# Four graph attention layers: VectorE's neighbour sums through a PSUM bank, and ScalarE's row copy behind the next tile's norm

## The reference

```python
# --- layer 0 (adj_preln) ---
h = jnp.maximum(_layernorm(x, axis=-1), 0.0)
x = x + _L0_gnn_ref(h, adj, L0_gnn_W, L0_gnn_a)   # 4 heads: Wh = h @ W; softmax(leaky(s_i + s_j)) @ Wh; elu
h = jnp.maximum(_layernorm(x, axis=-1), 0.0)
x = x + _L1_gnn_ref(h, adj, L1_gnn_W, L1_gnn_a)   # 1 head: h @ W + softmax(...) @ h
h = jnp.maximum(_layernorm(x, axis=-1), 0.0)
x = x + _L2_gnn_ref(adj, h, L2_gnn_weights, L2_gnn_biases, L2_gnn_phis)   # 4 heads, biases, no elu
h = jnp.maximum(_layernorm(x, axis=-1), 0.0)
x = x + _L3_gnn_ref(h, adj, L3_gnn_Wq, L3_gnn_bq, L3_gnn_Wk, L3_gnn_bk, L3_gnn_Wv, L3_gnn_bv)   # q k v attention
```

## Time and profile before

| | us |
|---|---|
| median of 3 runs | 1858.07 |
| lowest and highest | 1850.53, 1858.45 |
| the profiled execution | 1857.89 |
| its span (first to last instruction) | 1856.1 |
| busy: GpSimd, VectorE, TensorE, ScalarE | 1183.0, 1276.6, 724.0, 638.4 |
| chain that ended last: GpSimd, issue, TensorE, VectorE | 53%, 18%, 9%, 8% |

### The profile page before, as it was taken

The page is one execution under the profiler, slowest core; times in us unless marked ns, Lnnn a source line. Parts: engine busy times, 40 slices in busy tenths (PEclk is TensorE's granted clock), DMA queues, the critical chain, the costliest instruction groups (busy, mean ns, idle before and its releaser), DMA issues.

```text
span 1856.1 us, 12880 instructions
## 1 busy us (share of the span) xinstructions
PE 724.0 (39%) x2660; PEld 407.7 (22%) x2660; DVE 1276.6 (69%) x2730; ACT 638.4 (34%) x2069; POOL 1183.0 (64%) x1201
## 2 busy tenths in 40 slices
PE   3565500112223312233345134555666233455354
PEld 2443300001111101111122011222222222334243
DVE  2887743978888929666778196677653639668684
ACT  6778500223334511112223123233333222423343
POOL 0000267777777777777777787777744654777774
PEclk9996555555555555555555566666666566776777
DMA  9999789444454464444455644455545665777773
GB/s 354 384 384 364 183 278 169 107 117 119 125 133 129 129 135 110 123 128 124 131 142 135 135 119 141 138 151 152 161 137 158 193 167 160 232 239 223 240 233 101
DMA packets 171212, 328.63 MB, mean 177 GB/s; under 512 B 39918, under 2 KB 82935, under 8 KB 171128
## 3 DMA queue, kind: packets, MB, share of 16 engines
q0 software_dynamic: 65920, 197.88, 39.4%
q1 hardware_dynamic: 82600, 104.48, 17.6%
q10 hardware_dynamic: 22608, 25.40, 4.0%
HBM read 288.94 MB, written 38.72 MB: 177 GB/s over the span
## 4 chain that ended last, share of the span: by engine, by line
POOL 53%; issue 18%; PE 9%; DVE 8%; ACT 6%; DMA 4%; SPq 1%; ACTq 1%; POOLq 0%; DVEq 0%
POOL s_ring L749 50%; PE ps L1575 3%; ACT s_a L804 2%; DMA s_adj<-in_adj_dram 2%; DMA s_ring<-s_tab,s_idx 2%; PE ps L1544 2%; POOL s_pay L736 1%; DVE s_sc L1286 1%; DVE s_ring L1284 1%; POOL out_dram L756 1%; PE ps L1580 1%; SPq L599 1%; PE ps L1600 1%; DVE s_ring L1395 1%; DVE s_ring L1399 1%
## 5 line engine op out<-in xcount | busy, mean ns | idle before, releaser
L749 POOL DMA_INDIRECT s_ring<-s_tab,s_idx x1104 | 1115.6, 1010 | 419.3 <-issue 337.3
L939 ACT ACTIVATE ps<-s_sc,s_least 128x9 f32<-128x9 f32 (+12 forms) x416 | 110.3, 265 | 701.5 <-DVE s_least L1272 461.1
L1395 DVE TENSOR_TENSOR s_ring<-s_ring,ps 128x2304 f32<-128x2304 f32 (+10 forms) x96 | 261.2, 2720 | 3.3
L1399 DVE TENSOR_TENSOR s_ring<-s_ring 128x512 f32<-128x512 f32 (+7 forms) x249 | 234.8, 943 | 8.6
L1555 PE MATMUL ps<-s_ident,s_hb 128*128 128x128 f32 x128 | 43.8, 446 | 415.9 <-ACT s_hb L895 359.9
L1600 PE MATMUL ps<-s_ring,s_ident 128*128 128x256 f32 x366 | 125.2, 511 | 202.9 <-DVE s_ring L1417 202.9
L736 POOL DMA_INDIRECT s_pay<-s_pay_t,s_rank_i x32 | 31.2, 974 | 223.0 <-DVE s_rank_f L1144 213.5
L1284 DVE TENSOR_TENSOR s_ring<-s_ring,ps 128x2304 f32<-128x2304 f32 (+12 forms) x32 | 87.1, 2721 | 123.6 <-DMA s_ring<-s_tab,s_idx 123.2
L1268 DVE SCALAR_TENSOR_TENSOR s_sc<-s_ring 128x36 f32<-128x36 f32 (+20 forms) x96 | 18.4, 192 | 186.9 <-DMA s_ring<-s_tab,s_idx 186.6
L1584 PE MATMUL ps<-s_wx,s_hT 128*128 128x258 f32 (+1 forms) x256 | 134.8, 682 | 30.9 <-ACT s_hT L904 29.8
L1600 PEld LDWEIGHTS ps<-s_ring,s_ident 128*128 128x128 f32 x366 | 92.6, 261 | 232.5 <-issue 214.4
(11 more groups left out here) (190 smaller groups left out, 1409.3 us busy)
## 6 DMA issues: line engine op xcount, KB each, us to landing
s_adj<-in_adj_dram SPq DMA_DIRECT2D x32, 2048.0 KB, 16.1
s_ring<-s_tab,s_idx POOLq DMA_INDIRECT x1104, 3.2
s_tab<-s_tb ACTq DMA_DIRECT2D x32, 256.0 KB, 2.5
s_ring<-s_tab SPq DMA_DIRECT2D x32, 256.0 KB, 3.7
s_ring<-s_pay SPq DMA_DIRECT2D x32, 132.0 KB, 2.3
s_tab<-s_tb ACTq DMA_DIRECT2D x32, 132.0 KB, 2.5
s_ring<-s_tab SPq DMA_DIRECT2D x32, 132.0 KB, 2.3
s_tab<-s_tb ACTq DMA_DIRECT2D x32, 129.0 KB, 2.4
```

The source lines that it names most:

```text
L749: e.indirect_dma_start(g[:, k, 0:L.row], None, table, bass.IndirectOffsetOnAxis(ap=self.idx[:, t, k:k + 1], axis=0)).then_inc(self.gat[n % ...
L939: m = e.activation(p[:, :, h], s[:, :, h], ACT.Exp, bias=self.least[:, j, h:h + 1], scale=-1.0, accum_out=self.total[:, j, h:h + 1])
L1395: e.tensor_tensor(v, v, wide(p, 3, L.hd), ALU.mult).then_inc(self.v)
L1399: e.tensor_tensor(g[:, 0:h, :], g[:, 0:h, :], g[:, c - h:c, :], ALU.add).then_inc(self.v)
```

## The change

`vec_sum` no longer adds by halves in SBUF. It multiplies the first two rows into PSUM bank 2 (`two`, 2 x 256), the others in place as before, and then adds the others to the bank, two rows (512 elements) at a time; an odd row is added alone. In layers 1 and 2 the bank's two halves stay apart and `vec_finish` adds each to `x`. In layer 0 three adds of 256 elements bring them together, since the elu needs the whole sum. On ScalarE `act_row(n-2)` moves behind `act_hidden(n-1)` and `act_turned(n-1)` in layers 0 to 2, and at a layer's end `act_turned(31)` goes ahead of `act_row(30)`.

```diff
     def total_y(self, L, n):
-        return self.half[:, n % 2, :] if L.n < 3 else self.bank(2 + n % 2, 0, D)
+        return self.bank(2 if L.n < 3 else 2 + n % 2, 0, D)
+
+    def two(self):
+        return self.bank(2).rearrange("p (k d) -> p k d", k=2)
...
-            if n > 1:
-                self.act_row(e, l, n - 2)
             if n:
                 self.act_hidden(e, l, n - 1)
                 self.act_turned(e, l, n - 1)
+            if n > 1:
+                self.act_row(e, l, n - 2)
         if l == 1:
             self.act_below(e, T - 1)
         if l < 4:
             self.act_hidden(e, l, T - 1)
+            self.act_turned(e, l, T - 1)
             self.act_row(e, l, T - 2)
-            self.act_turned(e, l, T - 1)
             self.act_row(e, l, T - 1)
...
-        v = g.rearrange("p k (h d) -> p k h d", h=L.heads)
-        e.tensor_tensor(v, v, wide(p, 3, L.hd), ALU.mult).then_inc(self.v)
-        while c > 2:
-            e.wait_ge(self.v, vs.up())
-            h = c // 2
-            e.tensor_tensor(g[:, 0:h, :], g[:, 0:h, :], g[:, c - h:c, :], ALU.add).then_inc(self.v)
-            c -= h
-        e.wait_ge(self.v, vs.up())
-        e.tensor_tensor(self.half[:, n % 2, :], g[:, 0, :], g[:, 1, :], ALU.add).then_inc(self.agg)
+        e.tensor_tensor(parted(two), parted(g[:, 0:2, :]), wide(p[:, 0:2], 3, L.hd), ALU.mult).then_inc(self.v)
+        vs.up()
+        v = parted(g[:, 2:c, :])
+        e.tensor_tensor(v, v, wide(p[:, 2:c], 3, L.hd), ALU.mult).then_inc(self.v)
+        vs.up()
+        if c % 2:
+            e.wait_ge(self.v, vs.n)
+            e.tensor_tensor(two[:, 0, :], two[:, 0, :], g[:, c - 1, :], ALU.add).then_inc(self.v)
+            vs.up()
+            c -= 1
+        for a in range(2, c - 2, 2):
+            e.wait_ge(self.v, vs.n)
+            e.tensor_tensor(two, two, g[:, a:a + 2, :], ALU.add).then_inc(self.v)
+            vs.up()
+        e.wait_ge(self.v, vs.n)
+        if L.n:
+            e.tensor_tensor(two, two, g[:, c - 2:c, :], ALU.add).then_inc(self.agg)
+            return
+        e.tensor_tensor(g[:, c - 1, :], two[:, 1, :], g[:, c - 1, :], ALU.add).then_inc(self.v)
+        e.tensor_tensor(two[:, 0, :], two[:, 0, :], g[:, c - 2, :], ALU.add).then_inc(self.v)
+        vs.up()
+        e.wait_ge(self.v, vs.up())
+        e.tensor_tensor(two[:, 0, :], two[:, 0, :], g[:, c - 1, :], ALU.add).then_inc(self.agg)
...
         elif L.n == 1:
-            e.scalar_tensor_tensor(x, y, self.total[:, n % 2, 0:1], x, ALU.mult, ALU.add).then_inc(self.x_new)
+            total = self.total[:, n % 2, 0:1]
+            e.scalar_tensor_tensor(x, y, total, x, ALU.mult, ALU.add).then_inc(self.v)
+            e.wait_ge(self.v, vs.up())
+            e.scalar_tensor_tensor(x, self.two()[:, 1, :], total, x, ALU.mult, ALU.add).then_inc(self.x_new)
+        elif L.n == 2:
+            e.tensor_tensor(x, x, y, ALU.add).then_inc(self.v)
+            e.wait_ge(self.v, vs.up())
+            e.tensor_tensor(x, x, self.two()[:, 1, :], ALU.add).then_inc(self.x_new)
```

More of the change, by code:

```diff
@@ L1388, in vec_sum @@
         vs, g, p = self.vs, self.rows(L, n)[:, :, 0:D], self.scores(L, n)[1]
-        c = KS[L.order[n]] + 1
+        c, two = KS[L.order[n]] + 1, self.two()
+        parted = lambda a: a.rearrange("p k (h d) -> p k h d", h=L.heads)
         if L.n == 1:
```

## The result

| | us | runs |
|---|---|---|
| before | 1857.61 median (1850.53 to 1858.45) | 4 |
| after | 1766.76 median (1766.33 to 1768.36) | 4 |
| ratio | 0.9521, 95% interval 0.9496 to 0.9545 | |
| the profiled execution of after | 1766.5, span 1764.7 | |

The account below looks back on a forecast made before the run. GpSimd's gathers, stalled by VectorE's two-SBUF-input adds, bound layers 1 and 2, VectorE layer 0, a ScalarE-TensorE loop layer 2's end. Layers 1, 2, 3 start 2.8, 23.7, 82.9 us earlier: 1857.9 - 82.9 = 1775 us, range 1762 to 1816.

Parts of the forecast that it names:

- The stall, and the gathers of 262 us: Layers 0 to 2: adds with two SBUF inputs stall gathers; with sums in PSUM, busy falls from 284-285 to near 262 us.
- Rival A: Gathers of layers 0 to 2: something other than the second SBUF input holds the port, stall stays; 1827 us, chance 0.08.
- Adds into PSUM at no extra cost: VectorE's 512-element adds into the bank: they stay near 0.69 us, 0 extra.
- rival B: VectorE's adds into PSUM cost 0.07 to 0.1 us more each; 1790 us, chance 0.13.
- rival D: VectorE's adds reading and writing the same bank take double, +0.53 us each; 1880 us, slower, chance 0.04.
- VectorE's +0.56 us a tile in layer 0: VectorE's sum in layer 0: added instructions and gaps make it longer, 19.6 us before tile 29.
- The start of a layer behind the copy of tile 27: Next layer's first gather: copy at most 5.9 us after tile 29's scores; layer 1 starts 2.8 us earlier, layer 2 23.7.
- The end of layer 2: Tail of layer 2: TensorE bounds it at 6.93 us a tile instead of 10.24; layer 3's gathers resume 82.9 us earlier.
- just in time: End of layer 2: GpSimd's 20 early gathers are done at 1357.6, before layer 3's gathers go on at 1359.2.
- Rival C: Tail of layer 2: a wait still ties the copy ahead of the norm, 10.24 us a tile; 1814 us, chance 0.05.

Follow-up runs that it names:

- sbuf_total_2: The changed kernel with its two running sums in an SBUF tile instead of a PSUM bank: 1796.66 us, ratio 0.9682 to the kernel before.
- order_27_2: The changed kernel with row copies ahead of the norm again in layers 0 and 1, and in layer 2 for tile 27 alone: 1760.43 us, ratio 0.9496.
- order_tail: The changed kernel with the row copy ahead of the norm again, except from tile 30 of layer 2 on: 1787.98 us, ratio 0.9643.
- sums_only: The changed kernel with ScalarE's order of before: ratios 1.0074, 1.0054 and 1.0022 on three chips where before takes 2139 to 2157 us.
- order_only: The kernel before with ScalarE's new order, sums still in SBUF: ratios 0.9789, 0.9789 and 0.9807 on three chips where before takes 2139 to 2157 us.

## Why the prediction was right

**The stall, and the gathers of 262 us: right.** Rival A is out, by after's windows and by `sbuf_total_2`. Of the seven long gathers that are left, four start inside instructions with two SBUF inputs that the change did not touch (three in the elu's part of the finish, L1447). The other three, 1.20 and twice 1.26 us, run beside a scalar instruction (L1360) and two casts. These have one input and take 768 elements in 0.55 us, where an add takes 0.96. So the second SBUF input explains nearly all long gathers, not every one. Of before's long ones none starts inside L1402, which the prediction named too: 24 gathers start in that add of 0.42 us, none over 0.95.

**Adds into PSUM at no extra cost: right.** The groups of after (busy us, mean ns):

```profile
L1410 DVE TENSOR_TENSOR ps<-ps,s_ring 128x512 f32<-128x512 f32 x246 | 171.9, 699 | 8.5
L1398 DVE TENSOR_TENSOR ps<-s_ring,ps 128x512 f32<-128x512 f32 x96 | 66.8, 696 | 3.3
...
L1405 DVE TENSOR_TENSOR ps<-ps,s_ring 128x256 f32<-128x256 f32 x48 | 20.7, 432 | 1.7
```

699 ns against 693 in SBUF, where rival B needed 763 to 793 and rival D from 1120 on. Reading and writing the same bank costs 6 ns at most. The 120 cycles of the Trainium skill (VectorE: DVE Perf Modes, the section on the TRN2 errata), 65 ns over the SBUF figure, are not in these rows.

**VectorE's +0.56 us a tile in layer 0: the term that was mis-sized.** I charged each added instruction its duration and 0.03 us. A tile of eight neighbours took 5.79 us from its multiply to the end of `vec_apart` before and takes 6.13 now, +0.34. The timeline of after, the end of such a tile's sum:

```profile
516.90 0.42 DVE L1416 TENSOR_TENSOR s_ring<-ps,s_ring 128x256 f32<-128x256 f32 x1
...
517.25 0.42 DVE L1417 TENSOR_TENSOR ps<-ps,s_ring 128x256 f32<-128x256 f32 x1
...
517.70 0.43 DVE L1420 TENSOR_TENSOR ps<-ps,s_ring 128x256 f32<-128x256 f32 x1
```

L1417 does not wait for L1416 and starts 0.35 us after it, before its end at 517.32; L1420 waits for both and starts 0.45 after. The two multiplies, also independent, stand 0.61 us apart with a duration of 0.70. An instruction that waits for none before it costs about 0.1 us less than its row: 0.22 us a tile in these two places, 6.4 us over 29 tiles. From the first tile's scores to tile 29's it took 305.8 us, forecast 312.5. The first came 0.9 us later than before, which the forecast had not (313.89 against 312.99), so tile 29's came at 619.68 instead of 625.5, 5.8 earlier. The timeline of before had it already, in its last add and the `vec_apart` behind it, 0.34 us apart:

```profile
507.68 0.42 DVE L1402 TENSOR_TENSOR s_half<-s_ring 128x256 f32<-128x256 f32 x1
508.02 0.41 DVE L1440 TENSOR_TENSOR s_xs<-s_xs,ps 128x256 f32<-128x256 f32 x1
```

I had taken the gap from chains of dependent adds only.

**The start of a layer behind the copy of tile 27: right, and a little too dear.** Timeline of after, scores of tile 29, copy, first gather:

```profile
619.68 0.18 DVE L1271 SCALAR_TENSOR_TENSOR s_sc<-s_ring 128x24 f32<-128x24 f32 x1
...
625.27 0.17 ACT L919 ACTIVATE s_tb<-ps 128x2 f32<-128x2 f32 x1
...
628.14 0.95 POOL L752 DMA_INDIRECT s_ring<-s_tab,s_idx  x1 [17.20 <-issue]
```

5.6 and 2.9 us, forecast 5.9 and 3.7: 1.1 us. With the 5.8 above that is the 6.9 us by which the forecast of layer 1 was short, and layers 2 and 3 carry it (6.8 and 7.1). GpSimd idles 17 us here: layer 0 is VectorE's, its only wait between 313.5 and 640 us is one of 0.2 us. `order_27_2` and `order_tail` show that the copy's place costs 3.3 to 4.8 us at this start.

**The end of layer 2: wrong in what bounds it and in its rate, and neither counted.** I gave TensorE 6.93 us a tile from the rows of before, above VectorE's 6.2 and the gathers' 6.25, and called GpSimd's 20 early gathers "just in time". The tiles start 5.2 to 6.2 us apart and follow the gathers and VectorE, not TensorE, whose last two projections start 4.4 us apart. Two projections of after and one of `order_tail`:

```profile
1315.72 2.69 PE L1600 MATMUL ps<-s_wx,s_hT 128*128 128x512 f32 x4 [0.47 <-ACT s_hT L907]
...
1321.94 1.98 PE L1600 MATMUL ps<-s_wx,s_hT 128*128 128x512 f32 x4 [0.47 <-ACT s_hT L907]
```

```profile
1324.26 3.78 PE L1602 MATMUL ps<-s_wx,s_hT 128*128 128x512 f32 x4 [0.47 <-ACT s_hT L907]
```

The same four matmuls take 1.98, 2.69 and 3.78 us. The granted clock was 1.00 in the first of these times (2.4 GHz), 0.71 in the second, and 0.50 (1.2 GHz) in the third, as in the 3.78 us of the earlier trace rows. TensorE was busy 76% of after's tail (1296 to 1342 us) at a mean granted clock of 0.89, and 65% of before's (1383 to 1440) at 0.68. So a duration taken from a stretch at the lower level was too long.

The last tile's copy then stood at 1341.62, and the gathers behind the early ones went on at 1352.05 with a gap of 0.30 us, no wait. The whole tail lies under the 20 early gathers, which end at 1351.74; the forecast had 1357.6, less the 6.9 us 1350.7. That the too slow tail did no harm is luck: in the forecast it ended 1.6 us behind the early gathers (1359.2 against 1357.6), so the boundary would have been nearly the same without it. Rival C, a copy still tied in front of the norm, is out: `order_tail` shows what that looks like, and after's 0.2 us of waits for ScalarE are not it.

## What to carry to other kernels

Where GpSimd's indirect DMAs bound a kernel, look for VectorE instructions with two SBUF inputs beside them: put an accumulator in PSUM, or, where there is none free, cut the longest of these instructions. Moving work behind the critical copy helps only while the loop takes longer than what feeds it; put it there from the tile at which that turns, and leave ahead the copies on which the next layer's start waits. (The tile is an inference from the two cadences; what ran is the new order in one whole layer, `order_27_2`.) When you price added instructions, ask of each whether it waits for the one before it.

## What the runs showed of the hardware

**On some chips VectorE's instructions come at a fixed pace in some tiles.** On three of the five chips of the experiments the kernel before took 2139 to 2157 us, and the sums in PSUM were no gain (`sums_only` 0.5 and 0.7% slower on two, level within its interval on the third). Many tiles are untouched there: those of eight neighbours in layer 0 take 9.50 us in `sums_only`, as in after. Others are stretched, mostly the same ones on each such chip but not in each program: in `sums_only` tiles 0 to 3 of layer 0, 2 to 7 of layers 1 and 2 take 21 to 45 us instead of 10 to 19, in `order_only` tiles 3 to 11 of layer 1. The timeline of VectorE in one of them (chip 3):

```profile
833.65 0.43 DVE L1047 BATCH_NORM_STATS2 s_stat<-s_xs 128x6 f32<-128x256 f32 x1 [0.23 <-DVE s_xs L1452]
835.05 0.18 DVE L1050 BATCH_NORM_AGGREGATE s_stat<-s_stat 128x2 f32<-128x6 f32 x1 [0.97 <-DVE s_stat L1047]
836.44 0.15 DVE L1052 TENSOR_SCALAR s_stat<-s_stat 128x1 f32<-128x1 f32 x1 [1.21 <-issue]
```

Some instructions start right behind the one before and others 2.7 us after it, but the mean comes to 1.4 us, while GpSimd keeps its 1.25 us a gather. So in these tiles VectorE's count of instructions sets the time. In layer 1 a stretched tile of `order_only`, 15 instructions with before's sums, takes 20.5 to 21.1 us, and one of `sums_only`, 18 or 19 instructions, mostly 24.5 to 26.6: about 1.4 us for each. Faster gathers are worth nothing there. The order still gives 2%. Why those chips do it, and in these tiles, stays open.

**A gather that starts inside an add with two SBUF inputs ends 0.8 us after it**, or 0.95 us after its own start if that is later: a stall of at most 0.52 us beside an add of 0.70, 1.3 beside one of 1.49, and 3.0 beside one of 3.36. Beside an add with an operand in PSUM there is none.
